# Attention scores in four column strips at once, router logits with the router weights stationary, and a new order of all calls

## The reference

```python
h = L0_tok_weight[x]                                   # gather
h = h + attention(layernorm(h), 16 heads of 16)         # softmax over the 8 rows of x
h = h + ffn(layernorm(h))

# attention, for each token column n and head: 8 x 8 scores
attn = softmax(SCALE * einsum('bld,bmd->blm', q, k)); out = einsum('blm,bmd->bld', attn, v)

# ffn: 16 routed experts (4 of 16, chosen in 2 of 4 groups) and a shared one of twice the width
scores = sigmoid(flat @ Wg.T)
hid = relu2(einsum('th,eih->eti', flat, W1)); y = einsum('eti,ehi->eth', hid, W2)
out = einsum('eth,te->th', y, cw) + relu2(flat @ Ws1.T) @ Ws2.T
```

## Time and profile before

| | |
|---|---|
| median of 3 runs (lowest to highest) | 1297.22 us (1296.58 to 1298.7) |
| the profiled execution's own time | 1296.51 us |
| its span, first to last instruction | 1294.7 us |
| mean granted TensorE clock | 0.995 |
| PE busy / PEld busy | 1259.3 (97%) / 1037.6 us (80%) |
| DVE busy | 1022.7 us (79%) |
| ACT / POOL busy | 591.2 (46%) / 500.2 us (39%) |

### The profile page before, as it was taken

One profiled execution on the slowest core, in us unless ns is written; L12 is line 12 of the kernel. 1 busy time (PEld: TensorE's weight loads), 2 busy tenths in 40 slices (PEclk: granted clock), 3 DMA queues, 4 the chain that ended last, 5 costly groups with the idle time before them and its releaser, 6 DMA issues.

```text
span 1294.7 us, 19965 instructions
## 1 busy us (share of the span) xinstructions
PE 1259.3 (97%) x7556; PEld 1037.6 (80%) x7556; DVE 1022.7 (79%) x1732; ACT 591.2 (46%) x1040; POOL 500.2 (39%) x717
## 2 busy tenths in 40 slices
PE   4798999999999999999999999999999999999998
PEld 3467889797888979788797888979788797888987
DVE  4989787887878789787878878788787878978754
ACT  5234445444554544454353544544355354444443
POOL 6437254161623507253260724416262360705100
PEclk9899999999999999999999999999999999999999
DMA  6002222121321212122121322212122120212131
GB/s 217 1 17 83 66 83 82 35 82 49 99 66 55 94 33 97 52 83 82 34 86 45 100 66 82 71 46 82 50 89 76 51 92 29 94 49 83 66 107 57
DMA packets 34128, 91.66 MB, mean 71 GB/s; under 512 B 4720, under 2 KB 13296, under 8 KB 34032
## 3 DMA queue, kind: packets, MB, share of 16 engines
q1 hardware_dynamic: 30960, 81.99, 19.0%
q0 software_dynamic: 3072, 8.39, 2.5%
HBM read 81.46 MB, written 8.91 MB: 70 GB/s over the span
## 4 chain that ended last, share of the span: by engine, by line
PE 94%; DVE 3%; issue 1%; ACT 1%; POOL 1%; DMA 0%; DVEq 0%; POOLq 0%; SPq 0%
PE psY L1157 32%; PE psH L1142 30%; PE psB L1188 10%; PE psB L1203 9%; PE psA L1233 4%; PE psB L1221 2%; PE psA L1221 2%; PE psA L1245 2%; PE psB L1174 1%; PE psA L1174 1%; DVE ring L771 1%; PE psA L1254 1%; PE psY L1261 0%; DVE stats L754 0%; POOL xin L399 0%
## 5 line engine op out<-in xcount | busy, mean ns | idle before, releaser
L1157 PE MATMUL psY<-w_hi,hid_hi 128*128 128x256 f32 x1152 | 328.5, 285 | 0.0
L1157 PE MATMUL psY<-w_hi,hid_lo 128*128 128x256 f32 x1152 | 324.5, 282 | 0.0
L1157 PE MATMUL psY<-w_lo,hid_hi 128*128 128x256 f32 x1152 | 323.6, 281 | 0.0
L733 DVE SCALAR_TENSOR_TENSOR r_sb<-psH,cwB 128x512 f32<-128x512 f32 x256 | 174.8, 683 | 113.7 <-PE psH L1142 102.9
L533 ACT ACTIVATE hid_hi<-r_sb 128x512 fp32r<-128x512 f32 x288 | 179.8, 624 | 181.4 <-PE psY L1157 181.4
L1157 PEld LDWEIGHTS psY<-w_hi,hid_hi 128*128 128x128 f32 x1152 | 217.3, 189 | 31.4 <-issue 23.5
L1142 PE MATMUL psH<-xT_hi,w_hi 128*128 128x512 f32 x576 | 229.2, 398 | 1.4 <-DVE r_sb L733 1.4
L1142 PE MATMUL psH<-xT_hi,w_lo 128*128 128x512 f32 x576 | 227.4, 395 | 0.0
L1142 PE MATMUL psH<-xT_lo,w_hi 128*128 128x512 f32 x576 | 227.3, 395 | 0.0
L531 ACT ACTIVATE p_sb<-r_sb 128x512 f32<-128x512 f32 x288 | 180.2, 626 | 101.8 <-DVE r_sb L733 94.6
L1157 PEld LDWEIGHTS psY<-w_lo,hid_hi 128*128 128x128 f32 x1152 | 216.9, 188 | 8.1
(11 more groups left out here) (136 smaller groups left out, 1980.6 us busy)
## 6 DMA issues: line engine op xcount, KB each, us to landing
cwB<-cw_dram SPq DMA_DIRECT2D x128, 512.0 KB, 3.9
out<-h SPq DMA_DIRECT2D x32, 256.0 KB, 3.2
xin<-table,idx POOLq DMA_INDIRECT x64
ring<-w_t SPq DMA_DIRECT2D x4, 256.0 KB, 5.3
h<-w_t SPq DMA_DIRECT2D x2, 512.0 KB, 8.5
ring<-w_t SPq DMA_DIRECT2D x1, 512.0 KB, 5.9
p_sb<-w_t SPq DMA_DIRECT2D x2, 256.0 KB
cwB<-w_t SPq DMA_DIRECT2D x1, 512.0 KB
```

The source lines that it names most:

```text
L733: nc.vector.scalar_tensor_tensor(r_sb[:, n % 2, :], psH[:, n % 2, :], 0.0, cwB[:, (r // QN) % 2, r % QN, :], ALU.max, ALU.mult).then_inc(w ...
L1157: last = nc.tensor.matmul(psY[:, j // 2, (j % 2) * D:(j % 2 + 1) * D], hid[a][:, e % R, j * P:(j + 1) * P], W2[b][:, e, :], start=(e == 0 ...
```

## The change

Four things. The products are taken in another order, with both channel halves of a row pair next to each other (`lp, ih = t // KH, t % KH`). `score(b, lp)` now issues four matmuls, for both halves and both query rows, into the four strips at rows 0, 32, 64 and 96; there are as many matmuls as before. `logits` has the router weights stationary (128 columns of WGO: 32 of router weights and 96 of the output projection's, whose results are not used) and all 512 tokens moving, 4 matmuls; ACT copies 32 x 512 of the result (`logits_out`) into the upper part of cwT's tile, and PE turns it back by four transposes (`logits_back`). And the calls of all five engines stand in a new order, in the periods and in the start-up, with as many `warm(4)` calls as before.

```diff
-        WO = [sb(f"wo_{p}", [P, KH, D], f32r) for p in ("hi", "lo")]
-        WG = sb("wg_hi_lo", [P, KH, 2, E], f32r)
+        WGO = sb("wg_hi_lo_wo_hi", [P, KH, 2 * E + D], f32r)
+        WO = [WGO[:, :, 2 * E:2 * E + D], sb("wo_lo", [P, KH, D], f32r)]
...
-        cwT = sb("cwT", [E, T])
+        cwT = sb("cwT", [2 * E, T])
...
-            lp, ih = t % LP, t // LP
+            lp, ih = t // KH, t % KH
...
+            def logits_out(blk):
+                act.wait_ge(logit_mm, nth(blk, 1, 1))
+                wait(act, cwT_stored, nth(blk, 16, 0))
+                nc.scalar.copy(cwT[:, :], psA[0:2 * E, 0, :]).then_inc(lgT_ready, 1)
+
             def router(blk):
-                act.wait_ge(logit_mm, nth(blk, 1, 1))
+                act.wait_ge(lg_back, nth(blk, 1, 1))
                 wait(act, route_step, nth(blk, ROUTE_STEPS, 0))
                 nc.scalar.copy(lg[:, :, :, :].rearrange("p a b c -> p (a b c)"),
-                               psA[:, 0, 0:TT * 2 * E]).then_inc(lg_ready, 1)
+                               psA[:, 1, 0:TT * 2 * E]).then_inc(lg_ready, 1)
...
-            def score(blk, t):
-
-                lp, ih = t % LP, t // LP
-                pe.wait_ge(prod_ready[ih], nth(blk, LP, lp + 1))
-                if t == 0:
+            def score(blk, lp):
+
+                for ih in range(KH):
+                    pe.wait_ge(prod_ready[ih], nth(blk, LP, lp + 1))
+                if lp == 0:
...
-                for li in range(2):
-                    row = 64 * ih + 32 * li
-                    last = nc.tensor.matmul(psB[row:row + 32, 0, :], head_sum[:, lp, :], ring[:, t % 4, li, :],
-                                            start=(lp == 0), stop=(lp == LP - 1))
-                last.then_inc(score_mm, 1)
+                for ih in range(KH):
+                    for li in range(2):
+                        row = 64 * ih + 32 * li
+                        last = nc.tensor.matmul(psB[row:row + 32, 0, :], head_sum[:, lp, :],
+                                                ring[:, (KH * lp + ih) % 4, li, :],
+                                                start=(lp == 0), stop=(lp == LP - 1))
+                    last.then_inc(score_mm, 1)
...
             def logits(blk):
+
                 pe.wait_ge(xT_lo[1], nth(blk, 1, 1))
                 x = xT2[blk % 2]
+                for kh in range(KH):
+                    for a in range(2):
+                        last = nc.tensor.matmul(psA[:, 0, :], WGO[:, kh, 0:P], x[a][:, kh, :],
+                                                start=(kh == 0 and a == 0), stop=(kh == KH - 1 and a == 1))
+                last.then_inc(logit_mm, 1)
+
+            def logits_back(blk):
+                pe.wait_ge(lgT_ready, nth(blk, 1, 1))
                 for j in range(TT):
...
+                    last = nc.tensor.transpose(psA[:, 1, j * 2 * E:(j + 1) * 2 * E], cwT[:, j * P:(j + 1) * P],
+                                               ident[0:2 * E, 0:2 * E])
+                last.then_inc(lg_back, 1)
...
                 if b + 2 < B:
                     score(b + 2, 0)
                     score(b + 2, 1)
+                if b < B:
+                    up(b, 14)
```

334 lines of the change are left out of this document (163 added, 171 removed).

## The result

The changed kernel takes 1247.57 us (median of four runs, 1247.4 to 1247.62); the kernel before, on the same chip, 1296.9 us (1296.24 to 1298.7). The ratio is 0.9617, 95% interval 0.9601 to 0.9634. The forecast was 1244.5 us, with a range from 1238 to 1262: 3.1 us too low, and inside the range. The profiled execution lies 0.17 us under the median, where the forecast had put 0.7; the span itself was forecast 3.7 us too low.

The account below looks back on a forecast made before the run. PE's work was taken to bound the steady state. Scores 48.2, logits 3.0 and start-up 1.5 sum to 52.7 us off 1296.51, giving 1243.8, plus 0.7 for the median: 1244.5 us, range 1238 to 1262.

Parts of the forecast that it names:

- What bounds the kernel: Steady-state periods: PE is busy throughout, so one us of PE work removed from a period is one us gained.
- The scores: Score groups on PE: four strips side by side without loss, 3.44 us less per period, 48.2 us over 14 periods.
- Rivals 2: Score groups: four strips run only two at a time, groups stay at 3.76 us, total 1292.7 us; chance 0.06.
- rival 3: Score groups: four strips overlap with some loss, step 0.54 us, 12 us in all, total 1257 us; chance 0.05.
- The logits: Router logits on PE: 0.2 us saved per period, bounds 0 and 0.33, 3.0 us over 15 periods.
- Who could be late: Other engines in the periods: PE waits of zero to 0.3 us per period, none taken in the sum.
- Rival 1: Dense stretch: DVE becomes the bound, 0.3 to 1.5 us of waits per period, total 1249 to 1266 us; chance 0.20.
- Rival 4: Between `transpose_rows(1)` and `spread_probs(0)`: DVE's chain outlasts PE's 30 us by over 3.6, kernel slower, e.g. 1315 us; chance 0.03.
- The start-up: Stretch before period 0: 1.5 us gained, bounds -1 (a loss) and +4, period 0 starting 0.5 to 1 us earlier.
- the first values 1.7 us earlier: Start-up: with two weights' low parts moved behind, the first values, before at 48.26 us, come near 46.5 us.
- The tail: After block 15's weights: neither scores nor logits there, so no change.
- The sum: Whole kernel: 48.2 + 3.0 + 1.5 = 52.7 us off the profiled execution's 1296.51 us, median forecast 1244.5 us.

Follow-up runs that it names:

- experiment 1: Changed kernel with its new call order and logits, but products paired as before, so a score group has two strips; 1298.07 us.
- experiment 2: Changed kernel with the old logits (16 matmuls, tokens stationary, no copy, no way back) in the new call order; 1258.07 us.
- experiment 3: Kernel before with the new product pairing and four strips, old call order except the second product moved behind the seventh routing step; 1280.95 us.
- Experiment 9: Experiment 8 plus product 7 of block 1 before routing, one weight's low part into period 0, `up` 14 before the last logits' way back; 1245.53 us.
- experiment 5: Changed kernel with GpSimd's (POOL's) old start-up order, constants before block 1's gathers; 1247.64 us.
- experiment 10: Experiment 9 with GpSimd's old start-up order, the diff of experiment 5, added; 1245.08 us.
- experiment 8: Changed kernel, in the period without block b+2, `down` 9 put ahead of the transposes, `up` 13 and `down` 10 ahead of the logits; 1247.62 us.
- experiment 12: Experiment 10 with the weighing of experts 13 and 14 ahead of routing on DVE in the period without block b+2; 1243.23 us.
- experiment 4: Changed kernel with each score group's four half-0 matmuls issued first, then the four of half 1; 1249.51 us.
- experiment 6: Experiment 5 without the two fillers between the third and fourth projections of block 1; 1253.13 us.
- experiment 7: Changed kernel with five more fillers of four matmuls behind the last scores of block 0; 1249.14 us.

## Why the prediction came out as it did

**What bounds the kernel**: right. A us of PE's work in a period was a us of time, both ways: -3.94 with the change, +3.42 and +0.50 with its parts undone, PE busy throughout each time.

**The scores**: right, mechanism and size. The step with four strips is 0.43 us, no loss; the group costs 2.05 us for the 2.04 predicted; 3.44 per period stood in the sum, 3.42 was measured (experiment 1). Rivals 2 (two at a time) and 3 (some loss) fall. The Trainium skill gives 2.38 for three column tiles (TensorE: Matmul & The Clock Gate, Part 3, Measured speedup vs the span model). No run here has three, but the loss that rival 3 took from it did not come: four strips of float32 kept the step of two, 0.43 us.

**The logits**: mis-sized. 0.2 stood in the sum, with 0.33 as the upper bound; 0.50 was measured (experiment 2). The matmuls cost the 0.93 predicted. The mis-sized term is the way back, which adds 0.36 us for the 0.52 of the prediction: four transposes at 0.07 us, not 0.11, and one entry of 0.08 to 0.09. The 0.11 was read from transposes with 128 columns moving; here 32 move. 1.78 - 0.93 - 0.36 = 0.49 is what experiment 2 measured to 0.01. What the prediction feared as its lower bound, another entry and exit for 0.3 us, was that one entry. Together with the scores' 3.44 the period was predicted at 73.4 and came out at 73.13. Over 14 periods of 3.94 us, 55.2, against 48.2 and 14 x 0.2, this is 4.2 us more gain than the sum had.

**Who could be late**: right in the steady state, where nothing is, although the spare was counted in tenths. In the dense stretch, from the end of those transposes (365.45) to `spread_probs(0)` (394.85), PE has 29.4 us and DVE 25.6 us of work, so 3.8 us to spare where the prediction had some 2, and PE waits for nothing there. Rival 1 did not come: DVE has 10.6 us to spare in a period. Rival 4 did not come either, but experiment 3 shows its mechanism at work where the order is not adapted: 1.2 us of wait per period.

**The start-up**: wrong, and the sign too. 1.5 us of gain stood in the sum with a bound of one us lost; up to period 1 the after kernel is level with the one before although period 0 should have brought 3.94, so 3.9 us were lost. The step that failed is "the first values 1.7 us earlier". They came at 48.85 against 48.26, later. The chain from the first product to them did get shorter, by 2.8 us (29.90 to 48.85, before 26.50 to 48.26; of the 2.9 us of waits that the prediction counted there, 2.0 lie later, in block 1), but it starts 3.4 us later, and its start the prediction had not looked at. The start of period 0 was to come 0.5 to 1 us earlier; at the place on DVE where the prediction marks it, it went from 103.22 to 108.18.

After the first values, the prediction had named a right cause (the second attention's products need both halves of k) and gave it no price. Rows of DVE before, and then of the changed kernel:

```profile
74.89 1.41 DVE L754 BATCH_NORM_STATS2 stats<-h 128x6 f32<-128x256 f32 x4
84.03 1.21 DVE L760 TENSOR_TENSOR xT_lo<-psA,xT_hi 128x1024 fp32r<-128x1024 f32 x1
87.69 0.23 DVE L790 TENSOR_TENSOR lgt<-lg 128x64 f32<-128x64 f32 x1 [1.01 <-ACT lg L593]
```

```profile
76.07 1.41 DVE L760 BATCH_NORM_STATS2 stats<-h 128x6 f32<-128x256 f32 x4
79.98 5.77 DVE L288 TENSOR_TENSOR ring<-q_sb,k_sb 128x1024 f32<-128x1024 f32 x5 [2.50 <-ACT k_sb L567]
86.80 1.22 DVE L766 TENSOR_TENSOR xT_lo<-psA,xT_hi 128x1024 fp32r<-128x1024 f32 x1
91.46 1.13 DVE L796 TENSOR_TENSOR lgt<-lg 128x64 f32<-128x64 f32 x1 [1.17 <-ACT lg L601]
92.51 1.21 DVE L288 TENSOR_TENSOR ring<-q_sb,k_sb 128x1024 f32<-128x1024 f32 x1
```

Read as differences of the two traces, which a start-up repeats to about 1 us:

| up to | later than before, us | new in this part, us | what stands in it |
|---|---|---|---|
| statistics of block 0's residual | 1.2 | 1.2 | the late start of the chain, not all of it caught up |
| low part of the second transposed rows | 2.8 | 1.6 | DVE's wait of 2.50 us for k of half 1, and five products in a row |
| first routing step on DVE | 3.8 | 1.0 | the logits' way over ACT and back: 4.66 us from the low part, before 3.66 |
| the weights' transposes on PE (105.00, before 97.64) | 7.4 | 3.6 | the routing chain, 13.5 us instead of 10.0 |
| start of period 0 | 6.7 | -0.7 | |
| start of period 1, with the 3.9 us added that period 0 saves | 3.9 | -2.8 | before, period 0 took 3.0 us longer than the others, now 0.2 |

The third row is borne out by experiment 2, where the old logits take 3.66 us again (85.96 to 89.62). In the fourth row stand four things that were elsewhere before: product 7 (1.14), maxima and subtraction (1.33), the low part of the probabilities (1.41), and 0.9 us by which POOL's addition of the bias slows the first routing step (1.13 instead of 0.23 us, POOL's instruction from 89.98 to 92.50); against them a wait of 1.0 us for POOL is gone. Experiment 9 undoes the first of the four and gets 0.65 us. Experiments 5 and 10, which begin earlier and gain next to nothing by period 0, say that a late beginning is not the whole cause; they do not exclude it, since in 5 half the clock took 1.7 us of what had been won. How much of the 3.9 us would come back if each part were undone alone stays open, and so does what the clock drops took in the parts ahead of the routing (0.50 of full for 20.4 us in this trace, 10.2 before): each edit moved the drops.

**The tail**: wrong by 2.5 us, 2.3 longer where the sum had 0.2 less for block 15's logits. "No change" took it that the last part has neither scores nor logits; but it begins with period 14, which has the logits of block 15 and the new order, and there the calls of block b+2 that the new order counts on as cover are missing. The list of waits in the earlier trace rows could not show it, but the order of PE's calls without those of b+2 does: transposes, one `down`, logits. That the order is the cause and not the strips or the logits, three experiments show: the last part is 114.0 us in the new order without the four strips (experiment 1), 115.8 in the new order with the old logits (experiment 2), and 111.7 in the old order with the strips (experiment 3). Experiments 8, 9 and 12 show it step by step: two waits of 2.3 us go, come back as 0.9, then as 1.5, and go for good once the weighing moves too.

**The sum**: 52.7 us were predicted off the span and 49.0 came. The periods gave 4.2 more, the start-up 5.4 less (1.5 and 3.9) and the tail 2.5 less: 52.7 + 4.2 - 5.4 - 2.5 = 49.0. So errors of 4.2 and 7.9 us went against each other: that the total came within 3.1 us is in part luck.

## What to carry to other kernels

Cost a change to a periodic kernel in four places, not one: the period, the way in, the first and the last period, in which calls are missing that elsewhere cover a wait. When products of two halves are paired so that matmuls fill all strips of the array, ask when the first pair can exist, since that is what the start-up pays. And before closing a gap on VectorE look at what GpSimd does in it.

## What the runs showed of the hardware

- Matmuls with 32 output rows in four strips run at no loss against two: 16 float32 records of 512 columns in four steps of 0.43 us, against eight steps with two strips. The strips need not alternate in the program: with the other two strips' matmuls eight records further back, the step stayed 0.43 and the fours stayed (experiment 4).
- The entry into such a group costs about 0.09 us and the exit 0.11. A group of four small transposes directly ahead (32 rows, 32 columns moving) has a step of 0.07 us and an entry of 0.09 of its own, and the score group behind it still pays 0.08.
- POOL's instructions of four columns took 0.20 us beside an idle DVE and 1.06 to 1.21 us beside a run of products from SBUF (experiment 6; 1.03 to 1.20 in experiment 3). In the start-up of the changed kernel it went the other way round as well: a DVE instruction that takes 1.22 us took 2.35 beside POOL's addition of the bias, and the first routing step 1.13 instead of 0.23.
- Fillers on TensorE held the granted clock where they stood and did not keep it from dropping 50 us later (experiment 7). Half the clock between the weights' transposes and period 0 made that stretch 4.0 to 4.5 us long instead of 2.8.
